# Local attention in a 25-stage kernel: sine products on VectorE and their sums on GpSimd, three slots behind the projection in place of two

## The chip, the cores and the metric

The program runs on one core of a Trainium2 chip, as one launch. A core has TensorE (matrix products, PE in the views), VectorE (DVE), ScalarE (ACT), GpSimd (POOL) and SyncE (SP, which here only issues transfers). Each engine works through its own instructions in the order in which they were written down and waits at semaphores for the others. The metric is the time of one execution on the device in microseconds (us), as the median of several.

## The reference

The reference is a chain of 16 blocks on a residual `x` of 4 x 512 rows by 128 (attention, feed-forward and state-space blocks). One of them is used twice, `_L1_ffn_ref`: two layers of local attention with rotary positions. Cut to what matters here:

```python
def rotate_half(x):
    x1, x2 = jnp.split(x, 2, axis=-1)
    return jnp.concatenate([-x2, x1], axis=-1)
...
    q = q * cos * scale + rotate_half(q) * sin * scale
    k = k * cos / scale + rotate_half(k) * sin / scale
...
def _layer(x, wqkv, qs, ksc, wo, lg, lb, w1, b1, w2, b2):
    qkv = shift_token(x) @ wqkv            # 2 x 1024 rows, 8 heads of 64
    q = l2norm(q) * qs; k = l2norm(k) * ksc
    q, k = rotary_xpos(q, k)
    o = local_attention(q, k, v)           # windows of 64, each sees itself and the one before
    x = x + o @ wo
    ... layer norm, h @ w1, a * gelu(g), @ w2, added to x
```

## The kernel before, in words

The stages run in the order of `PLAN`. Each engine has one function per stage. `l1f_pe`, `l1f_act`, `l1f_dve`, `l1f_pool` and `l1f_sp` do both layers of the local attention in one go, and the plan has them twice; these two executions are called pass one and pass two here (on the trace from about 700 to 1170 us and from about 1650 to 2090 us).

A pass has 8 groups of projections (4 stretches of 512 rows in each of 2 layers) and 128 units of attention (16 for a group). The order is written out by hand in slots: `SLOTS = range(-16, 142)`, and each engine's function is a loop over the slots. Slots -16 to -1 are called the lead-in. In slot `u` of 0 to 127 one unit of attention (two heads, 128 queries) begins:

- PE computes its scores (L1838 to L1842), VectorE adds the mask and takes the maximum (L1986), ScalarE takes the exponential (L1928), VectorE the reciprocal (L1994), GpSimd multiplies by it (L2059), PE transposes two slots later (L1897), VectorE copies that (L2040), and PE multiplies by the values (L1851, L1853).
- PE's scores of slot `u` wait for VectorE's mask step of slot `u - 1`, and VectorE's mask step of slot `u` waits for PE's scores of slot `u`. So the two engines run at most about one slot apart.

The projections of the next group and the feed-forward part of an earlier one are laid into the same slots by `l1f_dense`. With `n = slot % 16`, the eight projections `a` of a group (`ITEMS`: four of the keys, then four of the queries; number `j`) stand at n = 0, 1, 2, 3, 5, 6, 9 and 10. For each of them:

- PE multiplies (L512); ScalarE copies the product to `RAW` (L519) and squares it (L1939).
- SyncE issues four transfers that swap blocks of 32 partitions from `RAW` into the tile `TP` (`swap`, L2090; `swap_in` tells of the landing). Between the swaps it issues the transfers of shifted values (L2096, L2099).
- VectorE, one slot behind, multiplies the product by the cosine table (L516, `AR<-PS,WS`, called the cosine product here).
- VectorE, two slots behind, multiplies the swapped tile in place by the sine table (L516, `TP<-TP,WS`, the sine product), after it has waited for the landing.
- GpSimd, two slots behind, adds that to the cosine product (L2066, the sum; `head_sum`).

Other work of VectorE in a slot n matters too: root steps, the Newton steps for the norms, each of three short instructions that depend on one another, of which L737 is the first (n = 5, 6, 7 for the keys and n = 12, 13, 14 for the queries, always at the end of the slot; L733 starts a root in n = 5 and 12); the products of the keys with the spread norms (`wide`, L2016: two at n = 13, one each at 14 and 15); a layer norm at n = 15 and 0 (L586, L590, L597; from the third group on); the product with `wo` on PE in n = 4 (from the second group on), and its addition on VectorE in n = 5 (L2019); from the third group on (slot 39) the gate, `gate`/`up`, in n = 7, with the gelu on ScalarE (L1954), which needs another activation table than the exponential does.

The order inside a slot of VectorE's loop is: mask step, reciprocal, cosine product and other work of `l1f_dense(u - 1)`, sine product, first part of the gate, copy of the transposed unit (L2040), second part of the gate, root step.

A sum frees its part of `TP`: `swap` for item j waits in SyncE's queue for the sum of item j - 4. Scores of a group wait for the last sum of its projections.

Of the kernel before, what the change touches and what calls it, by code (L numbers as in the profile page):

```python
# [306 lines left out]
def drain(steps):  # L307
    for _ in steps:
        pass
# [139 lines left out]
def program(nc, plan, wall, half, pad, xin, out):  # L449
    where, _ = places(plan)  # L450
    ctx = ExitStack()
    with ctx:
# [30 lines left out]
        def slot(k, n=512):  # L483
            return TP[:, 512 * k:512 * k + n]

        def big(k, n=1):
            return AR[:, 2048 * k:2048 * (k + n)]
# [27 lines left out]
        def stt(e, o, a, s, b, f1, f2):  # L515
            return e.scalar_tensor_tensor(out=o, in0=a, scalar=s, in1=b, op0=f1, op1=f2)  # L516
# [85 lines left out]
        def ln_pool(e, w, k, chunks, gap=0):  # L602
            share = 1.0 / 128.0 if len(chunks) == 4 else 1.0
            for c in chunks:
                _, mean, rstd = ln_stats(c)
                w.wait_ge(*F.ln_moments.on((k, c)))
                e.tensor_scalar(rstd, mean[:, :, 1], share, 1e-5, ALU.mult, ALU.add).then_inc(*F.pool_step.up())  # L607
                w.wait_ge(*F.pool_step.newest())
                e.tensor_tensor(rstd, rstd, C("MHALF")[:, 0:4], ALU.pow).then_inc(*F.ln_rstd.up((k, c)))  # L609
            for _ in range(3 + gap):  # L610
                yield
# [1080 lines left out]
        def ln_slot(q):  # L1692
            return 16 * q + 30 if q < 7 else 134

        def gate_slot(q):
            return 16 * q + 39 if q < 6 else (133, 138)[q - 6]

        def down_slot(q):
            return gate_slot(q) + (2 if q == 6 else 1)

        def l1f_dense(slot_):

            g, n = slot_ // 16 + 1, slot_ % 16
            first, second = [], []
            if 3 <= g and slot_ - 3 in [ln_slot(q) for q in range(8)]:
                first += [("back", q, 0) for q in range(8) if ln_slot(q) + 3 == slot_]
            if g < 8:
                for j, at in enumerate((0, 1, 2, 3, 5, 6, 9, 10)):  # L1710
                    if n == at:
                        first += [("a", g, j)]
                second = [("norm", g, j) for j, at in enumerate((2, 3, 4, 4, 6, 7, 10, 11)) if n == at] + second
                if n == 11:
                    first += [("turn", g, 0)]
                if n == 12 and g:
                    first += [("wide", g, 0)]
                    second += [("wide", g, 1)]
                if n == 13:
                    first += [("wide", g, 2 if g else 0)]  # L1720
                    second += [] if g else [("wide", g, 1)]
                if n == 14:
                    first += [("wide", g, 3 if g else 2)]
                    second += [] if g else [("wide", g, 3)]
                second += [("v", g, j) for j, at in enumerate((8, 11, 13, 15) if g else (8, 11, 12, 12)) if n == at]
            for q in range(8):
                if slot_ == 16 * q + 20:
                    first += [("wo", q, 0)]
                if slot_ == ln_slot(q):
                    second += [("ln", q, 0)]  # L1730
                if slot_ == gate_slot(q):
                    first += [("gate", q, 0), ("up", q, 0), ("gate", q, 1)]
                    second += [("up", q, 1), ("gate", q, 2), ("up", q, 2)]
                if slot_ == down_slot(q):
                    first += [("down", q, 0)]
            return first, second
# [6 lines left out]
        def unit(u):  # L1743
            g, n = u // 16, u % 16
            return g, n // 4, n % 4
# [5 lines left out]
        def shift_dve(e, w, k, src, ready, c):  # L1751
            h, first = big(1), 512 * c + (1 if c % 2 == 0 else 0)
            w.wait_ge(*ready)
            if c % 2 == 0:
                e.memset(h[64:128, 512 * c:512 * c + 1], 0.0)
            e.tensor_copy(h[64:128, first:512 * c + 512], src[64:128, first - 1:512 * c + 511]).then_inc(*F.half_shifted.up(k))
# [204 lines left out]
        def l1f_dve(e, w, s, W0):  # L1961
# [13 lines left out]
            for u in SLOTS:  # L1975
                if u == 48:
                    begin(w, s + 1)
                if 0 <= u < UNITS:
                    g, r, i = unit(u)
# [16 lines left out]
                for item in first + second:  # L1996
                    name, g, j = item
# [25 lines left out]
                    if name == "down":  # L2023
# [2 lines left out]
                        stt(e, x[:, cs(c)], bank(at[item]), W(g)("b2"), x1[:, cs(c)], ALU.add, ALU.add).then_inc(*done.up((s + g // 4, c)))  # L2026
                        if g < 4:
                            shift_dve(e, w, (s, 0, g + 4), x, done.on((s, g)), c)
                for name, g, j in l1f_dense(u - 2)[0] if u > -15 else []:
                    if name == "a":  # L2030
                        _, _, scale, _, table, _ = PROJ[ITEMS[j][1]]
                        w.wait_ge(*swap_in[j % 4].on((s, g, j)))
                        stt(e, slot(4 + j % 4), slot(4 + j % 4), W(g)(scale), W(g)(table)[:, cs(g % 2)], ALU.mult, ALU.mult).then_inc(*F.head_sin.up((s, g, j)))
# [11 lines left out]
                g, n = u // 16 + 1, u % 16  # L2045
# [8 lines left out]
        def l1f_pool(e, w, s, W0):  # L2054
            for u in SLOTS:
                if 0 <= u - 1 < UNITS:
                    nm, pw = NM[(u - 1) % 8], PW[(u - 1) % 4]
                    w.wait_ge(*F.win_recip.on((s, u - 1)))
                    e.tensor_tensor(pw, pw, nm[:, 4:6].unsqueeze(2).to_broadcast([128, 2, 128]), ALU.mult).then_inc(*F.win_p.up((s, u - 1)))  # L2059
                first, second = l1f_dense(u - 1) if u > -16 else ([], [])  # L2060
                for name, g, j in l1f_dense(u - 2)[0] if u > -15 else []:
                    if name == "a":
                        r, z = ITEMS[j]
                        d = PROJ[z][5][:, r, g % 2, :]
                        w.wait_ge(*F.head_sin.on((s, g, j)))
                        e.tensor_tensor(d, d, slot(4 + j % 4), ALU.add).then_inc(*F.head_sum.up((s, g, j)))  # L2066
                for name, g, j in second:
                    if name == "ln":
                        drain(ln_pool(e, w, (s, g), [g % 4]))
                if 0 <= u < UNITS and u % 32 == 1:  # L2070
                    g = u // 16
                    w.wait_ge(*F.head_k.on((s, g, 3)))
                    w.wait_ge(*F.head_v_copied.on((s, g, 3)))
                    if g:
                        w.wait_ge(*F.win_pv.on((s, 16 * g - 4)))
                    e.tensor_copy(KB, KH[:, :, 0, 448:512]).then_inc(*F.head_tail.up((s, g + 1)))
                for q in range(4, 8):
                    if u == down_slot(q) + 2 or (q == 7 and u == SLOTS[-1]):
                        c = q % 4
                        w.wait_ge(*F.geglu_x.on((s + 1, c)))  # L2080
                        e.tensor_tensor(X[:, cs(c)], X[:, cs(c)], big(0)[:, cs(c)], ALU.add).then_inc(*x_done[c].up(s + 1))
# [961 lines left out]
        def dve_main(e):  # L3043
            w, F.engine = Waits(e), "dve"
            preamble(w)
            body = {"L0a": l0a_dve, "L0f": l0f_dve, "L0b": l0b_dve, "L1a": l1a_dve, "L1f0": l1f_dve, "L1b": l1b_dve,
                    "L2a": l2a_dve, "L2f": l2f_dve, "L2m": l2m_dve, "L3f": l3f_dve, "L3l": l3l_dve}
            for s, sec in enumerate(plan):
                if sec == "L3a0":
                    interleave([layers_dve(e, w, s, c) for c in ALL])  # L3050
                if sec.startswith("L3a") or sec == "L1f1":
                    continue
                head_dve(e, w, s)
                body[sec](e, w, s, begin(w, s))

        def pool_main(e):
            w, F.engine = Waits(e), "pool"
            e.memset(MBT[:, :], 0.0)
            preamble(w)
            body = {"L0a": l0a_pool, "L0f": l0f_pool, "L0b": l0b_pool, "L1a": l1a_pool, "L1f0": l1f_pool, "L1b": l1b_pool,  # L3060
                    "L2a": l2a_pool, "L2f": l2f_pool, "L2m": l2m_pool, "L3f": l3f_pool, "L3l": l3l_pool}
            for s, sec in enumerate(plan):
                if sec == "L3a0":
                    l3a_pool(e, w, s)
                if sec.startswith("L3a") or sec == "L1f1":
                    continue
                head_pool(e, w, s)
                body[sec](e, w, s, begin(w, s))
# [54 lines left out]
```

## Time and profile before

| | us |
|---|---|
| median of 3 executions | 4387.26 |
| lowest and highest of the 3 | 4381.35 and 4872.67 |
| the profiled execution, its own time | 4381.53 |
| the profiled execution, its span from first to last instruction | 4379.8 |
| mean clock granted to TensorE in it | 0.918 of full speed |

The profile is of one execution. Its time is that of the lowest run within 0.2 us, and what lies around the span is 1.7 us. The median is 5.7 us above it.

### The profile page before, as it was taken

The page shows a single profiled execution, that of the slowest core. Times are in us where ns is not written, and L with a number is a line of the kernel's source. Part 1 is how long each engine was busy: PE and PEld are TensorE (multiplying, and loading weights), DVE is VectorE, ACT ScalarE, POOL GpSimd, SP SyncE. Part 2 cuts the span into 40 slices and gives each one's busy share as a digit, 9 for nine tenths or more (in the row PEclk, how much of TensorE's full clock was granted, in tenths as well). Part 3 has the DMA queues.
Part 4 walks back from the last instruction along what each step waited for, and adds up shares of the span by engine and source line. Part 5 has one row for each costly group of instructions (what it writes and reads, how often), then busy time and mean ns, then how long its engine had stood idle before and what let it go on. Part 6 is the DMA issues. An engine that isn't in the chain of part 4 may idle for free.

```text
span 4379.8 us, 63073 instructions
## 1 busy us (share of the span) xinstructions
PE 3866.0 (88%) x22574; PEld 1863.3 (43%) x22576; DVE 2956.8 (68%) x7834; ACT 2377.7 (54%) x4077; POOL 1260.1 (29%) x1851
## 2 busy tenths in 40 slices
PE   8899968999889988998886888999998999969999
PEld 5222335555422235555552235555554334433343
DVE  4899665777589967777446984666667863378732
ACT  3477743566447765666446654454543773327732
POOL 1100022333220013333023872111114323433334
PEclk8799978899979998999987998999997999979999
DMA  1100002222020012221000000000001100011000
GB/s 56 25 20 16 15 35 77 58 57 58 18 64 19 16 48 64 57 56 44 6 11 0 0 9 9 9 18 9 18 32 27 29 11 0 32 25 25 15 0 10
DMA packets 57937, 120.47 MB, mean 28 GB/s; under 512 B 17140, under 2 KB 17140, under 8 KB 56344
## 3 DMA queue, kind: packets, MB, share of 16 engines
q1 hardware_dynamic: 56472, 114.87, 9.9%
q8 instruction: 179, 2.93, 0.3%
q10 hardware_dynamic: 1152, 1.57, 0.2%
q14 instruction: 134, 1.10, 0.1%
HBM read 40.88 MB, written 1.05 MB: 10 GB/s over the span
## 4 chain that ended last, share of the span: by engine, by line
PE 54%; DVE 26%; ACT 6%; POOL 5%; issue 5%; SPq 2%; DMA 1%; ACTq 0%; POOLq 0%; DVEq 0%
PE PS L512 31%; DVE SM L1275 7%; PE PS L1185 7%; PE PS L1137 5%; PE PS L2782 3%; DVE AR L516 2%; PE PS L1167 2%; PE PS L539 1%; SPq L2090 1%; POOL SV L609 1%; DVE AR L2582 1%; DVE AR L597 1%; DVE AR L1986 1%; PE PS L2425 1%; DVE TP L1272 1%
## 5 line engine op out<-in xcount | busy, mean ns | idle before, releaser
L512 PE MATMUL PS<-AR,WS 128*128 128x512 f32 (+1 forms) x2112 | 1050.2, 636 | 75.2 <-DVE AR L516 28.7
L1237 ACT ACTIVATE AR<-PS 128x1024 f32<-128x1024 f32 (+3 forms) x896 | 788.8, 931 | 205.3 <-PE PS L1167 201.2
L1275 DVE TENSOR_REDUCE SM<-PS 128x1 f32<-128x512 f32 x1280 | 803.1, 683 | 72.9 <-PE PS L1137 71.6
L519 ACT ACTIVATE AR<-PS 128x512 f32<-128x512 f32 (+6 forms) x568 | 358.4, 635 | 512.1 <-PE PS L512 422.1
L512 PEld LDWEIGHTS PS<-AR,WS 128*128 128x128 f32 (+1 forms) x2112 | 399.1, 200 | 528.1 <-issue 400.1
L1137 PE MATMUL PS<-AR 51*128 51x512 bf16 (+3 forms) x1792 | 508.2, 383 | 62.6 <-DVE SM L1275 15.9
L1185 PE MATMUL PS<-AR 128*32 128x512 f32 (+3 forms) x3584 | 447.2, 571 | 2.5 <-POOL AR L1327 1.9
L1928 ACT ACTIVATE AR<-AR,SM 128x128 f32<-128x128 f32 x512 | 248.0, 486 | 265.1 <-DVE SM L516 262.3
L1137 PEld LDWEIGHTS PS<-AR 51*128 51x128 bf16 x1792 | 133.2, 94 | 598.5 <-DVE SM L1275 404.4
L1167 PE MATMUL PS<-AR 51*128 51x512 bf16 (+3 forms) x1792 | 288.7, 366 | 8.3 <-ACT AR L1237 5.3
L512 PE MATMUL PS<-AR,H 115*115 115x128 bf16 (+3 forms) x912 | 219.1, 314 | 72.8 <-POOL MBT L1319 14.4
L2059 POOL TENSOR_TENSOR AR<-AR,SM 128x256 f32<-128x256 f32 x256 | 162.7, 636 | 380.7 <-DVE SM L1994 362.2
L1313 POOL CAST MBT<-SM 128x8 bf16<-128x8 f32 x128 | 28.2, 220 | 832.0 <-DVE SM L1278 691.2
L607 POOL TENSOR_SCALAR SV<-LNS 128x4 f32<-128x4 f32 x148 | 28.8, 194 | 816.9 <-DVE LNS L590 560.1
L2856 DVE TENSOR_TENSOR AR<-AR,PS 128x512 f32<-128x512 f32 x128 | 87.4, 687 | 255.2 <-PE PS L512 255.2
L1272 DVE CUSTOM_DVE_ANT_0 TP<-PS,H 128x384 f32<-128x384 f32 (+3 forms) x512 | 226.1, 486 | 41.0 <-PE PS L1137 35.7
L516 DVE SCALAR_TENSOR_TENSOR AR<-PS,WS,AR 128x512 f32<-128x512 f32 x148 | 109.7, 747 | 186.5 <-PE PS L512 159.1
L2870 POOL TENSOR_TENSOR AR<-AR 128x512 f32<-128x512 f32 x128 | 159.4, 1268 | 230.0 <-ACT AR L519 230.0
L512 PE MATMUL PS<-AR 128*128 128x16 f32 (+3 forms) x920 | 196.0, 363 | 27.9 <-DVE AR L914 10.9
L2066 POOL TENSOR_TENSOR AR<-AR,TP 128x512 f32<-128x512 f32 x128 | 162.2, 1267 | 183.5 <-DVE TP L516 183.5
L512 PE MATMUL PS<-WS,AR 128*128 128x256 f32 (+4 forms) x640 | 194.5, 445 | 18.8 <-DVE TP L516 9.2
L512 PEld LDWEIGHTS PS<-AR,H 115*115 115x115 bf16 (+3 forms) x912 | 97.3, 121 | 243.1 <-POOL MBT L1319 48.0
(321 smaller groups left out, 6888.4 us busy)
## 6 DMA issues: line engine op xcount, KB each, us to landing
TP<-RAW SPq DMA_DIRECT2D x512, 64.0 KB, 2.0
AR<-AR SPq DMA_DIRECT2D x720, 32.0 KB
VXT<-AR SPq DMA_DIRECT2D x120, 128.0 KB, 2.4
WS<-wall SPq DMA_DIRECT2D x4, 3654.5 KB, 11.2
WS<-wall SPq DMA_DIRECT2D x8, 902.5 KB, 4.4
WS<-wall SPq DMA_DIRECT2D x2, 3334.5 KB, 10.8
WS<-wall SPq DMA_DIRECT2D x1, 2384.0 KB, 9.1
WS<-wall SPq DMA_DIRECT2D x1, 1543.5 KB, 6.1
```

What stands on the lines that cost most here:

```text
L512: t = e.matmul(o, l, r, start=(n == 0), stop=(n == len(pairs) - 1))
L516: return e.scalar_tensor_tensor(out=o, in0=a, scalar=s, in1=b, op0=f1, op1=f2)
L519: return e.activation(o, i, ACT.Copy, scale=1.0)
L1137: e.matmul(bank(p, m), l, r, start=True, stop=True).then_inc(*F.at_scores_max.up((s, k, i, rr, k0, g)))
L1167: t = e.matmul(sv[:, g, off:512], l, r, start=True, stop=True)
L1185: t = e.matmul(bank(7)[32 * j:32 * j + 32, t0:t1], V[:, 8 * b + kti, v0:v0 + 32], pv[:, j % 2, t0:t1], start=(kti == 0), stop=(kti == nk - 1))
L1237: e.activation(pv[:, :, off:512], sv[:, :, off:512], ACT.Exp, scale=scale).then_inc(*F.at_exp.up((s, u, p2)))
L1272: e.tensor_tensor_reduce(out=slot(5 + len(masked) % 3, m), in0=bank(ring(n + g), m), in1=H["MASKED"][:, 512 - m:512], scale=1.0, scalar=-3 ...
L1275: e.tensor_reduce(top, bank(ring(n + g), m), AX.X, ALU.max).then_inc(*F.at_max.up((s, k, i, rr, k0, g)))
L1928: t = e.activation(pw[:, z, :], pw[:, z, :], ACT.Exp, bias=nm[:, 2 + z:3 + z], scale=rq[:, z:z + 1], accum_out=nm[:, 4 + z:5 + z])
L2059: e.tensor_tensor(pw, pw, nm[:, 4:6].unsqueeze(2).to_broadcast([128, 2, 128]), ALU.mult).then_inc(*F.win_p.up((s, u - 1)))
L2066: e.tensor_tensor(d, d, slot(4 + j % 4), ALU.add).then_inc(*F.head_sum.up((s, g, j)))
```

## The change

In the loops of VectorE and of GpSimd, the sine product and the sum of a projection stand three slots behind it in place of two. The place inside a slot is the same, and no instruction is added or taken away.

```diff
-                for name, g, j in l1f_dense(u - 2)[0] if u > -15 else []:
+                for name, g, j in l1f_dense(u - 3)[0] if u > -14 else []:
                     if name == "a":
                         _, _, scale, _, table, _ = PROJ[ITEMS[j][1]]
                         w.wait_ge(*swap_in[j % 4].on((s, g, j)))
...
                 first, second = l1f_dense(u - 1) if u > -16 else ([], [])
-                for name, g, j in l1f_dense(u - 2)[0] if u > -15 else []:
+                for name, g, j in l1f_dense(u - 3)[0] if u > -14 else []:
                     if name == "a":
                         r, z = ITEMS[j]
                         d = PROJ[z][5][:, r, g % 2, :]
```

The slots (n) in which VectorE has a sine product, and GpSimd the sum behind it, are 2, 3, 4, 5, 7, 8, 11 and 12 before, and 3, 4, 5, 6, 8, 9, 12 and 13 after.

## Rows read from the trace of the kernel before

**Rows 1.** The page: span, and busy time of each engine

```profile
span 4379.8 us, 63073 instructions
...
PE 3866.0 (88%) x22574; PEld 1863.3 (43%) x22576; DVE 2956.8 (68%) x7834; ACT 2377.7 (54%) x4077; POOL 1260.1 (29%) x1851
```

**Rows 2.** Windows, pass one: length, then busy PE, PEld, DVE, ACT, POOL, granted clock

```profile
700.00:1170.00 470.00, 428.30 (x3809) 261.12 (x3810) 356.71 (x1402) 276.78 (x765) 174.56 (x213) 0.90 0.25 59
```

**Rows 3.** Waits of VectorE, pass one, then pass two: total, times, longest

```profile
DVE TP L516 <- DMA TP<-RAW: 28.8, 28, 2.8
...
DVE TP L516 <- DMA TP<-RAW: 23.2, 26, 2.0
```

**Rows 4.** Instructions by line, pass one: busy us, mean ns, idle before

```profile
L516 DVE SCALAR_TENSOR_TENSOR TP<-TP,WS 128x512 f32<-128x512 f32 x64 | 48.1, 751 | 28.9 <-DMA TP<-RAW 28.8
L737 DVE TENSOR_TENSOR SV<-SV 128x32 f32<-128x32 f32 x48 | 24.0, 501 | 0.0
...
L2066 POOL TENSOR_TENSOR AR<-AR,TP 128x512 f32<-128x512 f32 x64 | 81.1, 1268 | 93.6 <-DVE TP L516 93.6
```

**Rows 5.** Timeline of VectorE and GpSimd, slots 22 and 23 (n 6, 7)

```profile
816.20 0.28 DVE L1986 CUSTOM_DVE_ANT_0 AR<-PS,H 128x128 f32<-128x128 f32 x1
...
818.42 0.28 DVE L1986 CUSTOM_DVE_ANT_0 AR<-PS,H 128x128 f32<-128x128 f32 x1
...
819.76 0.74 DVE L516 SCALAR_TENSOR_TENSOR TP<-TP,WS 128x512 f32<-128x512 f32 x1
...
820.75 1.14 DVE L737 TENSOR_TENSOR SV<-SV 128x32 f32<-128x32 f32 x1
...
822.26 0.28 DVE L1986 CUSTOM_DVE_ANT_0 AR<-PS,H 128x128 f32<-128x128 f32 x1
...
820.58 1.27 POOL L2066 TENSOR_TENSOR AR<-AR,TP 128x512 f32<-128x512 f32 x1 [0.69 <-DVE TP L516]
```

**Rows 6.** Timeline, slots 51 to 53 (n 3 to 5), PE's product with wo between

```profile
913.70 0.75 DVE L516 SCALAR_TENSOR_TENSOR TP<-TP,WS 128x512 f32<-128x512 f32 x1 [2.13 <-DMA TP<-RAW]
...
912.83 3.70 PE L512 MATMUL PS<-AR,WS 128*128 128x512 f32 x8
...
918.89 0.29 DVE L1986 CUSTOM_DVE_ANT_0 AR<-PS,H 128x128 f32<-128x128 f32 x1 [0.82 <-PE PS L1842]
```

**Rows 7.** Timeline, slots 4 and 21, and the lead-in: waits behind the swaps

```profile
750.18 0.66 PE L1897 MATMUL PS<-CS,AR 128*128 128x128 f32 x2 [1.76 <-DVE AR L2040]
...
813.69 0.75 DVE L516 SCALAR_TENSOR_TENSOR TP<-TP,WS 128x512 f32<-128x512 f32 x1 [1.31 <-DMA TP<-RAW]
...
710.13 0.75 DVE L516 SCALAR_TENSOR_TENSOR TP<-TP,WS 128x512 f32<-128x512 f32 x1 [0.94 <-DMA TP<-RAW]
```

**Rows 8.** Timeline, slot 39 (n 7) with a gate: ScalarE, then PE

```profile
870.91 0.49 ACT L1928 ACTIVATE AR<-AR,SM 128x128 f32<-128x128 f32 x1
...
871.99 1.28 ACT L1954 ACT_TABLE_LOAD   x1
873.28 1.26 ACT L1954 ACTIVATE AR<-PS,WS 128x512 f32<-128x512 f32 x2
...
874.02 2.84 PE L512 MATMUL PS<-AR,WS 128*128 128x512 f32 x6 [0.42 <-ACT AR L1954]
```

**Rows 9.** Timeline, slots 44 to 49 (n 12 to 1): VectorE, then PE

```profile
890.70 0.42 DVE L516 SCALAR_TENSOR_TENSOR SM<-SM 128x2 f32<-128x2 f32 x1
...
894.34 0.28 DVE L1986 CUSTOM_DVE_ANT_0 AR<-PS,H 128x128 f32<-128x128 f32 x1
...
896.55 0.18 DVE L737 TENSOR_TENSOR SV<-SV 128x32 f32<-128x32 f32 x1
...
897.10 0.28 DVE L1986 CUSTOM_DVE_ANT_0 AR<-PS,H 128x128 f32<-128x128 f32 x1
...
904.75 0.66 PE L539 MATMUL PS<-CS,AR 128*128 128x128 f32 x4 [1.03 <-DVE AR L597]
```

## The prediction

> **What bounds the kernel now.** I read the page first: PE is busy for 88% of the span [rows 1]. The change touches one stage alone, the local attention, which runs twice; so I took the windows of its passes. In pass one PE is busy for 428 of 470 us and VectorE for 357 [rows 2]: the stage is nearly full of PE work, some 42 us of it idle, and only what makes PE idle, or fills VectorE where PE already waits for it, can move the time. Pass two has the same pattern. Third, the waits: VectorE waits 28.8 us in pass one and 23.2 us in pass two for the swaps to land [rows 3], 52.0 us together, the largest sum among its waits. That is all that the change can remove. Fourth, the timeline slot by slot, each slot from the start of one mask step to the next. It shows who leads in which slot, the same in nearly every group:
>
> - n = 2 to 4: PE has no gap from the third group on; VectorE waits for swaps in n = 3 and 4, for the three slots before PE's long product with wo.
> - n = 5: VectorE has the more work and PE waits for it in n = 6.
> - n = 7 to 11: PE leads again; where there is a gate, ScalarE's gelu sits between.
> - n = 12 to 1: VectorE has no idle time, PE waits for it in nearly every slot. The last of those waits, 1.03 us, is for the layer norm [rows 9].
>
> **The change part by part.** No instruction is added or removed: 64 sine products and 64 sums a pass stay [rows 4]. Per group of 16 slots VectorE's sine products leave n = 2, 7 and 11 and come to n = 6, 9 and 13; in n = 3, 4, 5, 8 and 12 one stands before and after. GpSimd's sums go with them.
>
> *What a sine product costs in a slot.* 0.66 us of VectorE's time: it starts at 819.76 and the copy behind it at 820.42 (busy 0.74, of which the end overlaps the next). And there is a second cost. When it ends, GpSimd starts the sum of 1.27 us, here at 820.58. The root step at the end of that slot then takes 1.14 us for its first instruction, L737, and ends when the sum ends [rows 5]; in a slot without a sine product the same instruction takes 0.18 [rows 9]. So it is blocked for 0.96 us. The group by line agrees: 48 times 0.18 is 8.6 us, and 24.0 were used, which leaves 15.4 us, or 16 times 0.96 [rows 4]. The 16 of pass one are n = 5 and 12 in seven groups and n = 7 in the two that have no gate; never n = 6, 13 or 14. The two slots side by side give the whole price at once: slot 22 (n = 6, cosine product and root step) takes 818.42 - 816.20 = 2.22 us, slot 23 (n = 7, the same and a sine product) 822.26 - 818.42 = 3.84 us [rows 5]. The difference is 1.62 = 0.66 + 0.96.
>
> The Trainium skill ("SBUF — State Buffer", Who interferes with whom) says the same of a VectorE instruction with two SBUF inputs beside a GpSimd instruction that reads SBUF: the one that issues second is blocked until the first ends. L737 is such a one, and the trace agrees, with 0.96 us.
>
> *n = 13: +1.62 us, on the path.* It has a root step now without a sum beside it, and takes 897.10 - 894.34 = 2.76 us with two wide products [rows 9]. After the change it has the sine product and the sum too: 4.38. VectorE is the late engine from n = 12 to the layer norm, without idle time in between, so all of it reaches PE. 14 groups (7 a pass) give 22.7 us. Bounds: 0 if PE were the late one there, and 14 times 1.93 = 27.0 if a second short instruction beside the sum were held up by another 0.31. I take 22.7, since PE is seen waiting.
>
> *n = 12: -0.26 us.* Now the sum of n = 11 still runs into n = 12 and holds the bias instruction there at 0.42 us [rows 9], in place of 0.16; after the change n = 11 has none. The sine product and its blocked root step stay. 14 times 0.26 is -3.6 us. Bounds: 0 and -7 (when the wait for the landing in n = 11 is long, PE loses more than that).
>
> *n = 6, with a gate in n = 7: +1.3 us.* Slot 6 grows by 1.62, so the bias of slot 7, and with it the exponential that now starts at 870.91, the table load behind it at 871.99, the gelu at 873.28 and PE's next product, which waits for it until 874.02 [rows 8], all come later. ScalarE was itself busy for some 0.3 us after that bias was ready, so 1.3 us come through. The slots after it are PE's, so nothing is made up. Third to seventh group, 2 passes: 10 times 1.3 = 13.0 us. Bounds: 0 and 16.2.
>
> *n = 6 in the first two groups: 0.* The root step of n = 7 is freed by as much as that of n = 6 is blocked: 3.84 and 2.22 change places.
>
> *n = 9: 0.* VectorE has 0.66 us more there, and 0.66 less in n = 11, and it idles for 0.6 to 0.8 us before the mask step of n = 11. The cover is that idle time; if it were gone, it would be 14 times 0.66 = 9.2 us.
>
> *n = 2, 7 and 11 lose 0.66 us each.* In n = 2 and 11 PE leads, in n = 7 of the groups with a gate VectorE waits for the gelu. Nothing comes back but what stands above.
>
> *The waits for the swaps.* The landing times depend on SyncE's queue and hardly on VectorE; a slot is 2 to 4 us and the longest of these waits 2.8 [rows 3], so nearly all vanish. What they cost now is another matter. In slot 51 VectorE waits 2.13 us, until 913.70. PE meanwhile has its product with wo, 3.70 us from 912.83, and VectorE still waits 0.82 us for PE's scores at 918.89 [rows 6]. So these, most of the 52 us, cost nothing now. In the first group there is no product with wo yet, and PE waits there 1.76 us (and 1.1 a slot earlier) for the copy that stands behind the sine product [rows 7]: about 3 us come back in each pass, -6.0. In the second group 1.31 us of pass one are on the path [rows 7] and 0.8 in pass two: -2.1. In the lead-in the waits are 0.94 us [rows 7] and less, six of them; root steps and transfers stand in a chain there, and later sums block other root steps. Between -3 and +1.6 a pass I take -0.7: -1.4.
>
> *Other queues.* SyncE's swap of item j waits for the sum of j - 4. That sum is now at n = 3 for j = 4 (raw data at n = 5), 4 for 5, 5 for 6, 6 for 7 (raw at n = 10): at least two slots early still. Scores wait for the last sum at n = 13, three slots early. GpSimd's own products (L2059) stand before the sum in a slot as they did. No new wait.
>
> *Sum.* 22.7 - 3.6 + 13.0 - 6.0 - 2.1 - 1.4 = +22.6 us against the profiled 4381.5: 4404. The median of the runs shown is 5.7 us above that execution; I set the forecast between the two, at 4406 us, 0.4% slower.
>
> **The rivals.**
>
> *The waits decide (faster).* Its place is n = 12 to 1: if PE is really the bound there and its small gaps are only VectorE's jitter, n = 13 costs nothing, and n = 6 costs nothing if the exponential of slot 7 isn't what the gelu waits for. Then only the gains stay: -3.6 - 6.0 - 2.1 - 1.4 = -13.1, 4368 to 4374 us. It decides once n = 13 passes on less than 9.5 us in all, n = 6 none. For it speaks that VectorE is busy 76% of the pass only; against it the 1.03 us of PE's wait after that stretch [rows 9]. Chance 0.2.
>
> *All waits come back.* 4381.5 - 52.0 = 4330 us. This is what waiting as late as one can would give if nothing covered these waits. Against it speak the rows of slot 51 [rows 6]. Chance 0.02. The Trainium skill ("DMA: Bandwidth & Descriptors", Rules for kernel authors) advises just that: issue early, compute, and wait on the semaphore late. By that rule the change is a gain; whether the trace agrees hangs on which engine is late in those slots.
>
> *A half: no measurable change.* Only one of the two stretches passes its cost on, n = 13 or n = 6: +9.6 or -0.1. 4380 to 4394 us. Chance 0.16.
>
> *More than forecast.* The cover of n = 9 fails too (+9.2), the gate passes on all 1.62 (+3.2), n = 13 reaches its bound (+4.3), and the lead-in has its upper end (+4.6): 4406 + 21 = 4427 us. For it: short instructions of VectorE in n = 10 meet a sum as well. Chance 0.12.
>
> *It doesn't do what it says.* A deferred sum could hold back SyncE's queue and bring the same waits a slot later; the slack of two slots speaks against it. It would end near the third case, and is in its chance.
>
> **How the numbers follow.** Forecast 0.50 (4396 to 4416), faster 0.20, all waits 0.02, a half 0.16, more 0.12. The range from 4371 to 4428 us takes in all but the case of all waits, the tail of the last and part of the second. A measurement of this kernel can tell 2% from no change, that is 88 us: slower than 4475 or faster than 4300 is in no case, and I leave 0.01 for each: faster 0.01, same 0.98, slower 0.01.
>
> **What would show it.** VectorE's wait for `TP<-RAW` falls from 28.8 to under 10 us in pass one. L737 takes some 36 us in place of 24.0 (28 blocked in place of 16), with 1.14 in n = 5, 6, 12 and 13. Slot n = 13 goes from 2.76 to 4.4 us and n = 6 from 2.2 to 3.8; PE's waits for VectorE grow in n = 13 to 15. The whole difference lies in the two passes. I am wrong if n = 13 grows and PE's start in n = 1 doesn't come later against n = 12, or if n = 6 grows and the gelu does not.

## The result, and the profile after the change

The changed kernel takes 4432.64 us (median of 4 executions, 4431.20 to 4628.17), the kernel before 4385.35 beside it (4 executions): a ratio of 1.0111, with a 95% interval from 1.0093 to 1.0129. So it is 1.1% slower, where 0.4% was forecast, and 4.6 us past the upper end of the range. One execution of each (4628.17 and 4872.67) was disturbed; both medians have it in, the ratio leaves it out.

The page of the profile after the change, its span and the busy time of each engine [rows 1]:

```profile
span 4430.9 us, 63073 instructions
...
PE 3905.9 (88%) x22574; PEld 1880.9 (42%) x22576; DVE 2969.3 (67%) x7834; ACT 2377.8 (54%) x4077; POOL 1259.7 (28%) x1851
```

The count of instructions is the same, and yet PE is busy for 39.9 us more. Work that didn't change can only take longer if it runs slower. The windows show it. I cut each pass from the mask step of slot 0 to that of slot 127. First after (length; busy PE, PEld, DVE, ACT, POOL; granted clock; share and GB/s of the DMA engines), then before:

```profile
737.00:1181.40 444.40, 400.54 (x3655) 243.47 (x3653) 332.04 (x1329) 258.43 (x732) 162.54 (x200) 0.90 0.23 53
1674.10:2130.20 456.10, 412.01 (x3650) 250.12 (x3652) 331.39 (x1328) 259.18 (x732) 162.48 (x200) 0.87 0.22 51
```

```profile
738.90:1165.30 426.40, 392.86 (x3652) 241.75 (x3654) 325.85 (x1329) 258.90 (x732) 161.65 (x200) 0.91 0.24 55
1660.50:2077.20 416.70, 378.17 (x3652) 234.08 (x3654) 324.72 (x1329) 258.03 (x732) 161.97 (x200) 0.95 0.24 56
```

The passes grow by 18.0 and 39.4 us, 57.4 together. The two lead-ins, from the issue of the first swap to slot 0, shrink by 1.7 and 3.7 (32.7 and 34.7 us before), and the rest of the span, where nothing changed, by 0.8. The clock falls from 0.91 to 0.90 and from 0.95 to 0.87. The clock granted at any time is full (1.00, 2.4 GHz) or half (0.50, 1.2 GHz), so (1 - clock) x 2 x length is the time at half clock. From the clock records at full precision it goes from 119.5 to 212 us in the two passes together; I call it the half-clock time below. In n = 7 of the ten groups with a gate beside their projections (the third to the seventh of each pass) it goes from 5.9 to 42.5 us.

What the change was meant to remove is gone. Waits of VectorE, pass one [rows 3] (28.8 us before); pass two has 1.1 as well, for 23.2:

```profile
DVE AR L2040 <- PE PS L1897: 34.2, 30, 3.3
DVE AR L1986 <- PE PS L1842: 32.8, 31, 2.7
DVE AR L516 <- ACT TP L1939: 17.8, 21, 3.4
...
DVE TP L516 <- DMA TP<-RAW: 1.1, 2, 0.9
```

Instructions of VectorE by line, pass one [rows 4] (busy us, mean ns, idle before). L737 had 24.0 us:

```profile
L516 DVE SCALAR_TENSOR_TENSOR TP<-TP,WS 128x512 f32<-128x512 f32 x64 | 47.5, 742 | 1.2 <-DMA TP<-RAW 1.1
...
L737 DVE TENSOR_TENSOR SV<-SV 128x32 f32<-128x32 f32 x48 | 34.7, 722 | 0.0
```

Timeline of VectorE in a slot with n = 13, from one mask step (L1986) to the next [rows 9]:

```profile
951.31 0.28 DVE L1986 CUSTOM_DVE_ANT_0 AR<-PS,H 128x128 f32<-128x128 f32 x1
...
952.00 1.26 DVE L2016 TENSOR_TENSOR AR<-AR,PS 128x512 f32<-128x512 f32 x2
953.18 0.74 DVE L516 SCALAR_TENSOR_TENSOR TP<-TP,WS 128x512 f32<-128x512 f32 x1
953.85 0.41 DVE L2040 COPY AR<-PS 128x256 f32<-128x256 f32 x1
954.18 1.14 DVE L737 TENSOR_TENSOR SV<-SV 128x32 f32<-128x32 f32 x1
...
955.69 0.28 DVE L1986 CUSTOM_DVE_ANT_0 AR<-PS,H 128x128 f32<-128x128 f32 x1
```

955.69 - 951.31 is 4.38 us, to the digit what the prediction worked out. PE idles twice over it:

```profile
954.41 0.41 PE L1897 MATMUL PS<-CS,AR 128*128 128x128 f32 x2 [1.30 <-DVE AR L2040]
...
956.25 0.28 PE L1838 MATMUL PS<-AR 64*64 64x64 f32 x2 [1.00 <-DVE SM L1986]
```

The prediction missed what happens in n = 7 of a group with a gate. Timeline of VectorE in slots 70 and 71 of pass two (n = 6 and 7), then of PE:

```profile
1928.87 0.74 DVE L516 SCALAR_TENSOR_TENSOR TP<-TP,WS 128x512 f32<-128x512 f32 x1
1929.53 0.42 DVE L2040 COPY AR<-PS 128x256 f32<-128x256 f32 x1
1929.87 1.15 DVE L737 TENSOR_TENSOR SV<-SV 128x32 f32<-128x32 f32 x1
...
1931.38 0.28 DVE L1986 CUSTOM_DVE_ANT_0 AR<-PS,H 128x128 f32<-128x128 f32 x1
...
1932.07 0.73 DVE L516 SCALAR_TENSOR_TENSOR AR<-PS,WS 128x512 f32<-128x512 f32 x1
```

```profile
1928.85 1.98 PE L512 MATMUL PS<-AR,WS 128*128 128x512 f32 x4
1932.85 1.96 PE L512 MATMUL PS<-AR,WS 128*128 128x512 f32 x2 [2.02 <-DVE AR L516]
1934.60 0.63 PE L1897 MATMUL PS<-CS,AR 128*128 128x128 f32 x2
1935.03 1.71 PE L512 MATMUL PS<-CS,TP 128*128 128x2 f32 x8
1936.59 4.43 PE L512 MATMUL PS<-AR,WS 128*128 128x512 f32 x6
```

The same slot of PE before:

```profile
1896.59 1.98 PE L512 MATMUL PS<-AR,WS 128*128 128x512 f32 x4
1898.97 1.13 PE L512 MATMUL PS<-AR,WS 128*128 128x512 f32 x2 [0.39 <-DVE AR L516]
1899.93 0.38 PE L1897 MATMUL PS<-CS,AR 128*128 128x128 f32 x2
1900.15 0.95 PE L512 MATMUL PS<-CS,TP 128*128 128x2 f32 x8
1901.52 2.84 PE L512 MATMUL PS<-AR,WS 128*128 128x512 f32 x6 [0.42 <-ACT AR L1954]
```

Read them as a chain. Sine product and blocked root step make slot 6 longer by 1.62 us; the cosine product of slot 7 comes that much later; the second pair of PE's gate products waits for it, 2.02 us in place of 0.39. Then the same two products take 1.96 us in place of 1.13, and the eight small ones 1.71 in place of 0.95. Windows of this slot say why: ahead of it and in it after the change, behind it, and in it before (in a fence of its own).

```profile
1926.00:1933.00 7.00, 4.33 (x36) 2.59 (x36) 6.59 (x23) 3.54 (x12) 3.61 (x4) 1.00 0.29 69
1933.00:1939.80 6.80, 6.80 (x16) 3.95 (x17) 1.83 (x3) 2.73 (x5) 0.00 (x0) 0.50 0.04 9
1939.80:1945.00 5.20, 5.20 (x32) 2.51 (x31) 2.57 (x12) 3.03 (x6) 1.87 (x2) 1.00 0.00 0
```

```profile
1899.00:1905.80 6.80, 6.38 (x40) 3.53 (x41) 3.73 (x9) 4.99 (x7) 1.27 (x1) 1.00 0.15 33
```

The granted clock is full up to the end of the gap, half for the 6.8 us behind it, in which PE never idles and VectorE has only 1.83 us to do, and then full again (in four of these slots the stretch is 3.4 us long). From mask step to mask step slot 71 takes 10.90 us in place of 8.13. Of these 10 slots with a gate there are 7 in which such a stretch begins after the change, and none before; in two slots before, one that began in n = 6 runs on into n = 7. The Trainium skill ("TensorE: Matmul & The Clock Gate", Part 1) says that the clock is set by how busy the array has been recently; the trace agrees in that half clock follows the gap of 2.02 us.

### The profile page after: what moved, and what is told of

Read it like the earlier page. It is cut to its first block, busy times and chain, and to the rows that moved or that the text cites. A ratio compares the mean times of both kernels' runs of the same rounds, so it can differ in the third digit from the quotient of the medians.

```text
span 4430.9 us, 63073 instructions
## 1 busy us (share of the span) xinstructions
PE 3905.9 (88%) x22574; PEld 1880.9 (42%) x22576; DVE 2969.3 (67%) x7834; ACT 2377.8 (54%) x4077; POOL 1259.7 (28%) x1851
## 4 chain that ended last, share of the span: by engine, by line
PE 56%; DVE 27%; POOL 5%; ACT 5%; issue 5%; SPq 1%; DMA 1%; ACTq 0%; POOLq 0%; DVEq 0%
PE PS L512 32%; DVE SM L1275 7%; PE PS L1185 7%; PE PS L1137 5%; PE PS L2782 3%; DVE AR L516 2%; PE PS L1167 2%; PE PS L539 1%; DVE SV L737 1%; POOL SV L609 1%; DVE AR L2582 1%; DVE TP L516 1%; DVE AR L1986 1%; DVE AR L597 1%; PE PS L1897 1%
## 5 line engine op out<-in xcount | busy, mean ns | idle before, releaser
L512 PE MATMUL PS<-AR,WS 128*128 128x512 f32 (+1 forms) x2112 | 1069.8, 646 | 88.7 <-DVE AR L516 44.7
L1137 PE MATMUL PS<-AR 51*128 51x512 bf16 (+3 forms) x1792 | 508.8, 384 | 62.4 <-DVE SM L1275 15.9
L1272 DVE CUSTOM_DVE_ANT_0 TP<-PS,H 128x384 f32<-128x384 f32 (+3 forms) x512 | 226.2, 486 | 39.9 <-PE PS L1137 34.6
## 6 DMA issues: line engine op xcount, KB each, us to landing
WS<-wall SPq DMA_DIRECT2D x4, 3654.5 KB, 11.1
```

What stands on the lines that cost most here:

```text
L512: t = e.matmul(o, l, r, start=(n == 0), stop=(n == len(pairs) - 1))
L1137: e.matmul(bank(p, m), l, r, start=True, stop=True).then_inc(*F.at_scores_max.up((s, k, i, rr, k0, g)))
L1272: e.tensor_tensor_reduce(out=slot(5 + len(masked) % 3, m), in0=bank(ring(n + g), m), in1=H["MASKED"][:, 512 - m:512], scale=1.0, scalar=-3 ...
```

## The experiments

The first theory is therefore: 57.4 us in the passes are the slots that VectorE makes longer (n = 6, n = 13), and on top the clock that PE loses behind the gaps this opens. The rival without a clock: the longer slots alone, with more of them passed on than forecast. "Pass lengths" are from mask step to mask step as above, both passes together (before 843.0 us, after 900.4).

### The change taken apart: items 6 and 7, 0 to 3, 4 and 5

Both loops take their items from `behind(u)`, which moves only the items in `late`; 6 and 7 go to n = 12 and 13, 0 to 3 to n = 3 to 6, 4 and 5 to n = 8 and 9.

```diff
+        def behind(u):
+            two = l1f_dense(u - 2)[0] if u > -15 else []
+            three = l1f_dense(u - 3)[0] if u > -14 else []
+            late = (6, 7)
+            return [x for x in three if x[0] == "a" and x[2] in late] + [x for x in two if x[0] == "a" and x[2] not in late]
...
-                for name, g, j in l1f_dense(u - 2)[0] if u > -15 else []:
+                for name, g, j in behind(u):
```

Expected of items 6 and 7 alone: 

> The kernel before, with the sine products and sums of items 6 and 7 alone three slots behind (n = 11 and 12 become 12 and 13). My account (a sine product and its blocked root step enter the stretch n = 12 to 1, in which VectorE leads): n = 13 +1.62 us, n = 12 -0.2 us, 14 groups, so +19 us, 4404. Rival (the loss of the change comes with PE's gaps, behind which the chip grants half clock more often): +19 and as much again, 4415 to 4425, with more half-clock time in the passes than before (98 and 61 us). Second rival (PE leads there): within 5 us of before.

Expected of items 0 to 3 alone: 

> The kernel before, with items 0 to 3 alone three slots behind (n = 2 to 5 become 3 to 6; n = 7 keeps its sine product). My account without the clock: 10 slots n = 7 with a gate come 1.5 us later (+15), the first two groups lose 1.6 us in n = 6 four times (+6) and get 8 us of waits for swaps back, so +13 us, 4398. With the clock (PE gap of 2.0 us in n = 7 before the third gate product, half clock behind it): +25 to +35 us, 4410 to 4420. Rival (the waits for swaps were worth their 52 us): 4340.

Expected of items 4 and 5 alone: 

> The kernel before, with items 4 and 5 alone three slots behind (n = 7 and 8 become 8 and 9). My account: n = 7 of the first two groups gets 1.6 us back four times (-6), n = 9 to 11 lose 0.3 us in 14 groups (+4): 4383, no change. If the cover of n = 9 were missing altogether: +9, 4394.

| late items | median us | ratio to before, 95% | pass lengths against before | half-clock us (before 119.5) |
|---|---|---|---|---|
| 6 and 7 | 4403.48 | 1.0058 (1.0041 to 1.0075) | +19.7 | 113 |
| 0 to 3 | 4407.24 | 1.0056 (1.0035 to 1.0076) | +26.4 | 133 |
| 4 and 5 | 4381.06 | 1.0008 (0.9994 to 1.0022) | +0.2 | 109 |

Items 6 and 7 behave as predicted in their own slot: n = 13 is longer by 1.62 us in nearly every group, 21.9 in all. That the total fits too is in part luck: n = 0 is longer by 8.9 us besides, and slots 10 and 11 of pass one are shorter by 4.6, because the kernel before ran them at half clock. In items 0 to 3 lies the surprise. Slot 6 has its 1.63, but in 9 of 10 cases half clock begins in the slot with the gate behind it, and that slot is longer by another 1.4 to 2.65. The time lies between the two that were expected, without the clock and with it. With items 4 and 5 alone n = 9 grows by 0.55, n = 10 loses 0.3 to 0.4 and n = 11 grows by 0.4: no free swap, but what is left is below what a pass shows beside its other jitter. The three parts sum to 46.3 us, 11.1 less than the whole change.

### Root steps ahead of the sine product

```diff
+                if True:
+                    g, n = u // 16 + 1, u % 16
+                    if g < 8 and n in (5, 6, 7):
+                        next(roots[g, 1], None)
+                    if g < 8 and n in (12, 13, 14):
+                        next(roots[g, 0], None)
                 for name, g, j in l1f_dense(u - 3)[0] if u > -14 else []:
...
-                if g < 8 and n in (5, 6, 7):
-                    next(roots[g, 1], None)
-                if g < 8 and n in (12, 13, 14):
-                    next(roots[g, 0], None)
```

Expected: 

> The changed kernel, with the root step of a slot ahead of its sine product in place of behind it, so that no sum of GpSimd runs beside it. My account (half or more of the loss is the short instruction held up behind the sum): L737 at 0.18 us nearly everywhere, slots n = 5, 6, 12, 13 shorter by up to 0.96 each, 4380 to 4400 us. Rival (the 0.66 us of the sine product alone does it, or the copy that now stands later makes PE wait instead): 4425 to 4440.

On the changed kernel this gives 4402.04 us, 1.0053 (1.0036 to 1.0070) of before, with the passes 36.0 us shorter than after the change, just outside the 4380 to 4400 expected. The group of L737 in pass one, and the windows of the two passes:

```profile
L737 DVE TENSOR_TENSOR SV<-SV 128x32 f32<-128x32 f32 x48 | 10.2, 213 | 0.6
```

```profile
736.30:1171.90 435.60, 399.23 (x3650) 244.03 (x3651) 318.70 (x1328) 258.81 (x732) 162.68 (x200) 0.89 0.23 54
1667.90:2096.60 428.70, 388.68 (x3649) 238.62 (x3650) 318.20 (x1328) 258.28 (x731) 162.63 (x200) 0.92 0.23 54
```

The block is real: put before the sine product, hence before the sum that the sine product releases, L737 takes 0.21 us and never 1.14, and its group falls by 24.5 us. But the slots give back less than 0.96 each, some 0.83 in n = 5 and 12 and 0.55 in n = 6 and 13, and n = 8 and 14 grow by 0.5. In n = 7 the passes lose 3.6 and 11.4 us, though the edit moves hardly anything there: the gap in front of the gate's second pair is 1.09 us in nine of the ten slots in place of 2.02, half clock begins in only 1 of the 10, and the half-clock time falls from 212 to 164 us. So even this gain is in part one of the clock.

The same edit on the kernel before:

Expected: 

> The kernel before (two slots behind), with the root step ahead of the sine product. If a blocked root step costs its 0.96 us where VectorE leads: n = 12 and n = 5 shorter by 0.8 to 0.96, some of it lost again to the later copy, 4366 to 4376 against some 4381. If it is hidden: 4381.

4374.51 us, 0.9985 (0.9970 to 1.0001), pass lengths -4.3: inconclusive, at most a small gain.

### Only the sine products of items 0 and 1 late

`late = (0, 1)`: two of the long waits for swaps go, and no sine product enters n = 6, 9 or 13.

Expected: 

> The kernel before, with items 0 and 1 alone three slots behind (n = 2 and 3 become 3 and 4): the waits for swaps go in those slots, and nothing is moved into a stretch that VectorE leads. My account (these waits are worth 8 us in the first two groups and nothing elsewhere): 4371 to 4378. Rival (each microsecond waited is worth one): 4350 to 4360.

4383.02 us, 0.9999 (0.9989 to 1.0009), pass lengths -0.5. VectorE's waits for swaps fall to 15.1 and 17.4 us, by 19.5 in all, and the time doesn't move. Gains of up to 8 us were expected, from the first two groups; not even these came. These waits are covered.

### The gaps filled with work that nobody needs

Products of a constant with itself, into columns that nobody reads, are put where PE would idle: 14 ahead of the gate's second pair, in the first variant; in the second, 10 more in n = 13 ahead of the transposes. They cost PE time, so a theory of longer slots alone expects no gain.

```diff
+            def keep(n):
+                for _ in range(n):
+                    e.matmul(PS[:, 2304:2560], H["I"], H16[:, 0:256], start=True, stop=True)
...
+                        if name == "gate" and j == 1 and g < 5:
+                            keep(14)
...
+                    if u % 16 == 13 and u < 112:
+                        w.wait_ge(*free[4])
+                        keep(10)
```

Expected of the first (gate only): 

> The changed kernel, with 14 short products (128 x 256, bf16, about 1.5 us in all) that PE computes into unused columns of bank 4 in n = 7, where it now idles for 2.0 us before the second gate product; they only keep it busy. If that gap brings the half clock behind it (it follows in 7 of 10 such slots): the half-clock stretches that begin in n = 7 go, 8 to 15 us less than the changed kernel, 4417 to 4425. If the clock has nothing to do with the gap: 4430 or more.

Expected of the second (both): 

> As the one before, and 10 such products in n = 13, where PE idles for 1.3 us before its transposes. If gaps bring the half clock: half-clock time in the passes falls from 92 and 120 us to about that of the kernel before (79 and 41), 4405 to 4415, which leaves the structure's loss of about 30 us. If not: 4430 or more.

The first takes 4424.09 us (4415.37 to 4431.42), 1.0099 (1.0080 to 1.0118), passes 9.8 us shorter than after the change. The second takes 4401.66, 1.0058 (1.0038 to 1.0078), below the 4405 to 4415 expected; its passes are 25.8 us shorter, with a half-clock time of 92 in place of 212. The rest of its 31 us lies outside the passes, where nothing was edited. Its windows, the third in the slot of the gate, then PE's timeline there:

```profile
729.50:1167.50 438.00, 395.37 (x3788) 247.21 (x3790) 332.67 (x1328) 257.59 (x731) 162.86 (x200) 0.95 0.23 53
1663.90:2100.40 436.50, 394.44 (x3789) 246.99 (x3791) 331.79 (x1328) 257.82 (x731) 162.87 (x200) 0.95 0.23 53
1914.00:1919.10 5.10, 4.86 (x36) 2.70 (x35) 2.92 (x7) 3.54 (x5) 0.00 (x0) 1.00 0.00 0
```

```profile
1910.50 1.69 PE L1836 MATMUL PS<-H 128*128 128x256 bf16 x14
1912.68 1.12 PE L512 MATMUL PS<-AR,WS 128*128 128x512 f32 x2 [0.49 <-DVE AR L516]
...
1915.05 2.85 PE L512 MATMUL PS<-AR,WS 128*128 128x512 f32 x6 [0.24 <-ACT AR L1963]
```

PE has 133 and 139 recorded instructions more in a pass (140 were added) and is busy for less time (395.37 against 400.54, 394.44 against 412.01). The second pair still starts when the cosine product lets it; but it takes 1.12 us again, and the slot 7.95. VectorE's busy time is that of the changed kernel, and n = 6 and n = 13 are still longer by 1.63 and 1.62 us a group than before: nothing of the longer slots was cured, only the clock. Half clock begins in none of the 10 slots with a gate any more, in either variant. 31.6 us over the passes of before are left. Of the 15.9 us by which the second variant's passes are shorter than the first's, 7.7 are in n = 0, behind the gaps that it fills, and 4.5 in n = 11, ahead of them; why n = 11 gains is not shown.

The same kind of products as a control where PE has no such gap, in n = 8 and 10. They stand in seven groups of a pass each, so they are 168 a pass in place of 140:

```diff
+                    if u % 16 in (8, 10) and u < 112:
+                        keep(14 if u % 16 == 8 else 10)
```

Expected: 

> The changed kernel with the same 14 and 10 short products of PE, but where PE has no gap: before its transposes of n = 8 and n = 10. If it is the gaps that bring the half clock: the half-clock time of the passes stays near the changed kernel's 212 us, and the added work of some 2.6 us a group is paid, 4450 to 4470. Rival (more work of PE anywhere keeps the clock up): half-clock time falls to about 90 us as with the filled gaps, 4415 to 4440.

4442.24 us, 1.0141 (1.0115 to 1.0166): passes 17.8 us longer than after the change, with n = 8 longer by 9 us a pass and n = 10 by 7. The 28 extra ones of a pass account for little of it: n = 8 of the two groups without a gate is longer by 2.7 us in all. So the place decides, not that PE does more. The time is below the 4450 to 4470 expected, for half-clock time fell here too, by 34 us (to 177), which didn't pay for the products. Of these 34 us 15 are in n = 7 of the gates: PE comes late to six of the ten, so its gap there is only 0.34 to 1.40 us, and half clock begins behind none of the six. Behind the four gaps of 2.02 it begins three times.

### A gap without the change

The other way round: the kernel before, all sine products at their old places, with a gap made in n = 7. PE's second gate pair waits for the sum of item 4 of the group being projected, which ends later than the cosine product does.

```diff
                         if name == "gate":
                             w.wait_ge(*F.ln_out.on(((s, g), c)))
+                        if name == "gate" and j == 1 and g < 5:
+                            w.wait_ge(*F.head_sum.on((s, g + 3, 4)))
```

Expected: 

> The kernel before, in which PE waits before the second gate product (n = 7, five groups a pass) until GpSimd's sum of item 4 is done. No other engine's work is moved; PE gets a gap of about 2.0 us there as in the changed kernel, where it had 0.4. The later products cost about 1.6 us each, +16 us, 4397, if the clock does not follow. If a gap of that size brings the half clock by itself: most of these slots are followed by a half-clock stretch that begins in n = 7 (none now), and 4408 to 4418.

4407.54 us (4393.12 to 4419.82), 1.0059 (1.0043 to 1.0075), pass lengths +37.0, just below the 4408 to 4418 expected with the clock and well above the 4397 without. PE's timeline in one such slot, and the window behind the gap:

```profile
1926.51 1.13 PE L512 MATMUL PS<-AR,WS 128*128 128x512 f32 x2 [2.39 <-POOL AR L2068]
1927.48 0.38 PE L1899 MATMUL PS<-CS,AR 128*128 128x128 f32 x2
1927.69 1.26 PE L512 MATMUL PS<-CS,TP 128*128 128x2 f32 x8
1928.81 3.76 PE L512 MATMUL PS<-AR,WS 128*128 128x512 f32 x4
```

```profile
1928.30:1935.00 6.70, 6.70 (x24) 3.00 (x25) 1.45 (x4) 2.03 (x3) 0.00 (x0) 0.50 0.00 0
```

In 9 of the 10 slots half clock begins behind the gap, where before it began in none. Those slots are longer by 3.1 to 4.8 us. In the tenth PE came out of n = 6 at half clock and was late, so that its gap was only 0.81; the wait ended at the same point of the slot, no half clock followed, and the slot is longer by 1.42. So the gap costs 1.4 by itself, and 1.7 to 3.4 more by the clock behind it: n = 7 grows by 37.7 us in all, of which 14.2 are 10 times 1.42. This is the one run in which the clock is shown to be lost without any move of a sine product.

Counted by gap over the four kernels that have it (after the change, items 0 to 3, the control and this one), PE idled for 2.01 to 2.39 us ahead of the gate's second pair 30 times, and half clock began behind it 28 times. Behind the nine gaps of 1.09 us of the kernel with root steps first it began once.

### Towards a better kernel

Root steps first and only items 0 and 1 late, on the kernel before:

Expected: 

> The kernel before with items 0 and 1 alone three slots behind and the root steps ahead of the sine products: both edits that did not lose. Root steps first gave 4 us in the passes, the two late items 0 to 1: 4370 to 4378, at the edge of what can be told. If the two help each other in the first groups: 4365 to 4370.

4369.45 us against 4381.02, 0.9976 (0.9960 to 0.9993), pass lengths -10.0 (833.0). It is the fastest of all, faster than both kernels, and by only 0.24%. Each half alone gave nothing that could be told from no change.

Root steps first together with both fillings, on the changed kernel:

Expected: 

> The changed kernel with both cures: root steps ahead of the sine products (30 us by itself) and PE's gaps of n = 7 and 13 filled (31 us by itself). If one acts on VectorE's time and the other on the clock: 4380 to 4390, near the kernel before. If both act on the same loss: 4400.

4397.22 us (4387.39 to 4407.32), 1.0041 (1.0026 to 1.0056). Each cure alone had taken some 30 us off the changed kernel; both take 35. They largely cure the same thing: with the gaps filled, root steps first bring only 5.9 us in the passes. Had they worked through the length of VectorE's slots alone, they would have added up.

## Why the prediction was wrong

The sign was right, the size was not, and the step that failed is this: the prediction priced PE's delay at n = 6 and 7 by its length alone and gave the clock behind the gap no term. The slots say so: +22.6 us were worked out against the profiled execution, and the profiled executions differ by 51.1. I add up the slots of the two passes by group, once as the prediction's terms have them and twice as measured. The kernel with both gaps filled stands for the change without its clock, though it still has 92 us of half clock, where the kernel before has 119.5.

| groups | forecast | gaps filled | after |
|---|---|---|---|
| first | -3.3 | -4.7 | -4.8 |
| second | +0.6 | -0.8 | +2.6 |
| third to seventh (gate in n = 7) | +26.6 | +35.9 | +59.9 |
| eighth | 0 | +1.1 | -0.4 |
| both passes | +24.0 | +31.6 | +57.4 |

The terms in turn:

- *n = 13: +1.62, 22.7 us.* Right: 10.2 and 11.7 us in the two passes. L737 took 34.7 us in pass one where 36 were forecast, and the slot shown 4.38.
- *n = 12: -3.6.* Nearly right: -1.1 and -1.8.
- *n = 6 with a gate: +1.3 of 1.62, 13.0 us.* Wrong, and it is the step that failed, in its path and in what follows from it. The path named was the exponential, the table load and the gelu. But PE's late partner is the cosine product in n = 7, which the second gate pair waits for, so the 1.63 become idle time of PE ahead of long products. With the gap filled, n = 6 and 7 together cost 14.7 us in the ten groups, near the 13.0. As the change leaves it they cost 31.0: half clock follows, and n = 7 is longer than before by 2.47 to 2.78 us in four of the five groups of pass two. The 16.3 us between 14.7 and 31.0 are what the runs showed in place of nothing.
- *n = 6 and 7 in the first two groups: 0.* Right, +1.63 and -1.62.
- *n = 9: 0.* Nearly right. The cover (VectorE's idle time before n = 11) isn't whole: n = 9 to 11 cost 3.9 us in the ten groups with the gaps filled, between 0 and the 9.2 named for a cover that is gone. A term that the prediction lacks is n = 0, with 4.4 in the same groups; 1.8 of it is one slot that has 3.2 us of half clock, and the rest is unexplained.
- *Waits for the swaps: -6.0, -2.1, -1.4.* Right in kind: 4.1, 2.0 and 3.8 us. In the kernel with filled gaps n = 0 to 5, where the waits stood, give back 4.1 us in the first groups and 2.0 in the second ones, and the two lead-ins give back 3.8, hardly clear of their jitter (an untouched lead-in took 32.7 to 34.7 us in two kernels). Without n = 12 and 13 the first groups as a whole give back 7.6 us, but 5.0 of that are slots 10 and 11 of pass one, which the kernel before ran at half clock. The waits vanished (1.1 us left in each pass) and most were worth nothing: 19.5 us of them taken away alone, with items 0 and 1, moved the passes by 0.5.
- *The clock.* No step of the prediction has it. It is 25.8 us, the difference of the last two columns, 16.3 of it in the n = 7 of the gates and 7.5 in n = 11 over all groups. It is an estimate that can be off either way: the filling has a price of its own, which makes it too low, and takes away more half clock than the change had added (119 us against 92), which makes it too high. With it the forecast's 24.0 misses another 7.6 us of the passes; its largest parts are the 3.9 in n = 9 to 11 and the 4.4 in n = 0.

Of the rivals, "the waits decide" fell with the first run: items 6 and 7 alone, which is n = 13 and 12, cost the passes 19.7 us where 9.5 were the limit. "More than forecast", at 4427 us, came nearest in time but by other mechanisms: n = 13 didn't reach its upper bound and the lead-in didn't cost; only a part of the gate's and of n = 9's terms did occur, and none of them has the clock behind the gap.

What half clock costs depends on where it falls. In n = 7 of the gates the two measurements are near each other: 40 us of it less were worth 16.3 us with the gaps filled, and in the kernel with the added gap 47 us more came with 23.5 us (37.7 - 14.2) beyond the gap itself, so 0.4 to 0.5 us for each. Elsewhere the filling took away another 79 us for only 9.5. In the gate's slot PE has 6.8 us without a break; where VectorE leads, a slower PE has room, which I only argue. What stays open: why the half-clock time is so different between the two passes of one kernel (78.5 and 41.0 before), and why it fell in the control outside n = 7.

## What to carry over

When an edit lets PE idle, ask for two prices: the idle time, and the clock of the long products that stand right behind it. PE's busy time that grows with an unchanged count of instructions is the sign, and windows of a few us ahead of the gap and behind it settle it; dummy products in the gap separate the two prices. And a sum of waits, however large, is worth what it holds up: here 50 us of waits were removed for about 10 (4.1 + 2.0 + 3.8), and the instructions that took their place stood in the slots in which VectorE was already the late engine.

## What the runs showed of the hardware

- Gaps of 2.02 and 2.39 us in a stream of which PE is busy for about 90% were followed by 1.2 GHz in 28 of 30 cases over four kernels, gaps of 0.39 at the same place in none. With 1.69 us of dummy products in the gap no half clock began behind it in any of the 10.
- Adding products can shorten a kernel: 24 short ones in a group with a gate and 10 in one without, in gaps, took the changed kernel from 4432.64 to 4401.66 us, 25.8 of it in the passes; such products elsewhere took it to 4442.24.
- A VectorE instruction of 128x32 with two inputs in SBUF, 0.18 us by itself, takes 1.14 while GpSimd's sum runs, in 53 of 96 cases of the changed kernel and in none where it was issued ahead of that sum (0.21 in the mean there, but for three of 0.5 to 0.8 us in the lead-ins). As the prediction cites from the Trainium skill ("SBUF — State Buffer", Who interferes with whom), it is the second to issue that is held up; moved ahead, it isn't held up, and n = 8 and 14 grew by 0.5 us instead, so a part of the gain is lost.
